# Maxima six steps ahead of the cubics, their rows in four transfers, other set-up order, fills at a step's end

## The reference

```python
mod = (silu(c) @ wmod).reshape(8, 6, 1, -1)          # sa, ca, ga, sb, cb, gb
h = layernorm(x) * (1 + ca) + sa
q, k, v = split(h @ w_qkv.T)                          # 16 heads of 8
logits = q @ k.T * 8 ** -0.5
logits = logits - max(logits, axis=-1)
s = where(x >= 0, 1 + x*(1 + x/2*(1 + x/3)), 1 / (1 - x*(1 - x/2*(1 - x/3))))   # at x = logits
x = x + ga * ((s / sum(s)) @ v @ w_out.T + b_out)
h = layernorm(x) * (1 + cb) + sb                      # then three layers with weights of +1 and -1,
x = x + gb * ffn(h)                                   # 2*128 -> 512 -> 512 -> 128, relu times 2 between
```

## Time and profile before

| | us |
|---|---|
| median of 3 runs | 708.13 (706.61 to 709.72) |
| the profiled execution, its own time | 708.76 |
| its span | 706.9 |
| VectorE busy | 646.2 (91%) |
| TensorE busy (matmuls, modelled ends) | 627.4 (89%) |
| ScalarE, GpSimd busy | 598.8, 599.0 (85% each) |
| granted TensorE clock, mean share of full | 0.971 |

### The profile page before, as it was taken

The page is one execution under the profiler, slowest core; times in us unless marked ns, Lnnn a source line. Parts: engine busy times, 40 slices in busy tenths (PEclk is TensorE's granted clock), DMA queues, the critical chain, the costliest instruction groups (busy, mean ns, idle before and its releaser), DMA issues.

```text
span 706.9 us, 9679 instructions
## 1 busy us (share of the span) xinstructions
PE 627.4 (89%) x3019; PEld 244.5 (35%) x3019; DVE 646.2 (91%) x768; ACT 598.8 (85%) x606; POOL 599.0 (85%) x390
## 2 busy tenths in 40 slices
PE   7577787877789999899989999899989999997798
PEld 5222222223222344233423333233423343334266
DVE  6899988989999999999999999999999999998943
ACT  2647877978899999999999989999999989998932
POOL 7769777897989999899989999899989989798920
PEclk9579999999999999999999999999999999999999
DMA  7514112141124222141224122241125112101001
GB/s 206 160 46 165 48 51 61 54 149 32 55 58 144 81 58 73 48 159 32 57 76 168 50 58 75 60 167 41 40 61 172 53 54 72 54 10 27 17 12 30
DMA packets 37783, 53.61 MB, mean 76 GB/s; under 512 B 11308, under 2 KB 20804, under 8 KB 37732
## 3 DMA queue, kind: packets, MB, share of 16 engines
q1 hardware_dynamic: 36766, 51.81, 24.1%
q10 hardware_dynamic: 966, 1.19, 0.6%
HBM read 29.17 MB, written 18.36 MB: 67 GB/s over the span
## 4 chain that ended last, share of the span: by engine, by line
PE 56%; DVE 17%; ACT 12%; issue 11%; POOL 2%; SPq 1%; DMA 1%; ACTq 0%; DVEq 0%; POOLq 0%
PE MB L515 13%; PE OP L593 12%; PE Z L561 9%; PE SA L576 8%; DVE cub L966 8%; DVE mx L975 7%; ACT sq L720 5%; ACT prob L734 4%; PE MB L528 3%; PE MB L505 2%; PE MB L612 2%; PE MB L486 1%; PE OP L443 1%; DVE st L1012 1%; PE MB L493 1%
## 5 line engine op out<-in xcount | busy, mean ns | idle before, releaser
L1201 POOL TENSOR_TENSOR cub<-cub 128x2048 f32<-128x2048 f32 x127 | 456.8, 3602 | 48.4 <-DVE cub L966 48.1
L720 ACT ACTIVATE sq<-Z,shift 128x1024 f32<-128x1024 f32 x256 | 282.3, 1116 | 58.5 <-PE Z L561 56.8
L966 DVE SCALAR_TENSOR_TENSOR cub<-sq,Z 128x1024 f32<-128x1024 f32 x256 | 309.8, 1211 | 13.0 <-ACT sq L720 12.2
L975 DVE TENSOR_REDUCE mx<-SA 128x2 f32<-128x1024 f32 x248 | 301.9, 1217 | 15.6 <-PE SA L576 12.2
L734 ACT ACTIVATE prob<-cub 128x2048 f32<-128x2048 f32 x128 | 244.3, 1910 | 0.4 <-PE OP L593 0.4
L576 PE MATMUL SA<-KH,QL 64*128 64x512 f32 x496 | 121.1, 485 | 33.4 <-DVE mx L975 29.3
L561 PE MATMUL Z<-QH,KH 64*128 64x512 f32 x512 | 128.8, 499 | 17.7 <-DVE cub L966 16.5
L593 PE MATMUL OP<-prob,Vq 128*16 128x512 f32 x1024 | 136.6, 607 | 0.0
L561 PEld LDWEIGHTS Z<-QH,KH 64*128 64x128 f32 x512 | 48.4, 185 | 197.6 <-DVE cub L966 121.6
L515 PE MATMUL MB<-hid,W 128*128 128x512 f32 x192 | 108.0, 645 | 0.0
L576 PEld LDWEIGHTS SA<-KH,QL 64*128 64x128 f32 x496 | 47.4, 187 | 111.1 <-DVE mx L975 89.4
(11 more groups left out here) (205 smaller groups left out, 501.6 us busy)
## 6 DMA issues: line engine op xcount, KB each, us to landing
QL<-parts_q SPq DMA_DIRECT2D x62, 128.0 KB, 2.6
KH<-parts_k SPq DMA_DIRECT2D x62, 128.0 KB, 2.7
QH<-parts_q SPq DMA_DIRECT2D x62, 128.0 KB, 2.7
parts_q<-SQ SPq DMA_DIRECT2D x28, 256.0 KB, 2.5
parts_k<-SK SPq DMA_DIRECT2D x28, 256.0 KB, 2.7
QH<-mp SPq DMA_DIRECT2D x253, 2.0 KB
nd<-OT SPq DMA_DIRECT2D x124, 32.0 KB
out<-y SPq DMA_DIRECT2D x7, 256.0 KB, 2.8
```

Of the source, the lines that this page charges most:

```text
L720: nc.scalar.activation(sq[:, h, :], Z[:, h, :], ACT.Square, bias=shift[:, 0:1]).then_inc(s_sq, 1)
L966: nc.vector.scalar_tensor_tensor(cub[:, m % RING, h, :], sq[:, h, :], CUB_ADD, Z[:, h, :], ALU.add, ALU.mult).then_inc(s_cv, 1)
L975: nc.vector.tensor_reduce(to, unit_bank(m, u)[:, :, :], AX_X, ALU.max).then_inc(s_mx, 1)
L1201: nc.gpsimd.tensor_tensor(ff, ff, ff, ALU.mult).then_inc(s_fp, 1)
```

## The change

- `AHEAD` is 6 instead of 7, so the maxima of a group stand one step later in relation to the cubics; `LEAD` goes from 3 to 4, which leaves the reading of q and k in the same steps. The three stages of `of_maxima` stand together round the first maxima of the step, where they were spread over it.
- The rows of maxima sit in rows 1, 33, 65, 97 of `QH` instead of 1, 3, 65, 67; four transfers of 4 KB carry them (`M_DMAS`) instead of eight of 2 KB. For the first quad the SyncE queue issues two and ScalarE two.
- `FILL`: one step fewer in batches 0 and 1, each fill now at the end of the step, and from batch 0 on it has a second matmul of 256 columns.
- Set-up: two dummy matmuls fewer at the start and two ahead of the first q; the transposes of the condition before those of the weights; wq and wk are copied before the modulation. One batch more of x's statistics on ScalarE (`ON_VECTOR` 3), its squares in four parts of five tiles in the steps -2 to 1 (`SQUARES_AT`) instead of in step -10; the last 1 MB of x is loaded after the first quad of q. The weights of the first layer are made on GpSimd instead of VectorE, and GpSimd's gates come after them and after the means; `gate_rows` is issued in step -3, not -7; the late roots of the norm in step 3 of batch 0, not in step -4.
- End: `l1_3` of batch 6 has a bank of `Z` to itself and starts in step 128, VectorE's last square moves behind a copy of that step, `xbg` and `wog` change places with `w2g`, and `pe_tail` issues the four products that add x before the pick of the last quad.

The core of the diff:

```diff
-AHEAD = 7
+AHEAD = 6
-ON_VECTOR = 4
+ON_VECTOR = 3
+SQUARES_AT = (-2, -1, 0, 1)
-M_DMAS = 8
-LEAD = 3
+M_DMAS = 4
+LEAD = 4
...
-    ("l1_2", -2, [(2, "c", 4)]), ("l1_3", -2, [(4, "b", 2), (4, "c", 2)]), ("y", -2, [(5, "c", 3), (5, "d", 1)]),
+    ("l1_3", -2, [(0, "b", 3), (0, "c", 1)]), ("l1_2", -2, [(2, "c", 4)]), ("y", -2, [(5, "c", 3), (5, "d", 1)]),
...
-FILL |= {(0, n): ("k", 2) for n in range(2, 12)} | {(0, n): ("v", 2) for n in range(12, 16)}
-FILL |= {(1, n): ("k", 3) for n in range(2, 8)} | {(1, n): ("x1", 1) for n in range(9, 12)} | {(1, 12): ("v", 3)}
+FILL |= {(0, n): ("k", 2) for n in range(2, 11)} | {(0, n): ("v", 2) for n in range(12, 16)}
+FILL |= {(1, n): ("k", 3) for n in range(2, 8)} | {(1, n): ("x1", 1) for n in range(9, 11)} | {(1, 12): ("v", 3)}
...
                     nc.tensor.matmul(MB[:, :], ident[:, :], W1f[:, n % KC, :], start=True, stop=True)
+                    if b >= 0:
+                        nc.tensor.matmul(MB[:, 0:S // 2], ident[:, :], W1f[:, n % KC, 0:S // 2], start=True, stop=True)
...
             logits(m, 1)
-            fill()
             with_v(s)
...
             logits(m + 1, 0)
             misc("d")
+            fill()
...
+            if s in SQUARES_AT:
+                if s == SQUARES_AT[0]:
                     act.wait_ge(s_mean1, 1)
+                count = (B - ON_VECTOR) * TB // len(SQUARES_AT)
+                for i in range(SQUARES_AT.index(s) * count, (SQUARES_AT.index(s) + 1) * count):
+                    mm = nc.scalar.activation(scratch(i), tile_of_x(i), ACT.Square, bias=mean1[:, i:i + 1],
+                                              accum_out=sq1[:, i:i + 1])
...
             cubic(s, 0)
             of_maxima(m, 0)
+            of_maxima(m, 1)
             maxima(m, 0)
-            of_maxima(m, 1)
+            of_maxima(m, 2)
             split(b, n)
             if b == B - 1:
                 norm_late()
             cubic(s, 1)
-            of_maxima(m, 2)
             maxima(m, 1)
...
             pool_setup(pool)
-            pool_gates(pool)
+            first_layer(pool)
             norms_of_x(pool, False)
             means_for_scalar(pool)
+            pool_gates(pool)
...
-            if b == FIRST and n == 9:
-                sp.wait_ge(s_gate, 7)
-                sp.dma_start(gate_rows, g_row).then_inc(s_gw, 16)
...
+            if b == FIRST and n == 13:
+                sp.wait_ge(s_gate, 7)
+                sp.dma_start(gate_rows, g_row).then_inc(s_gw, 16)
...
         def pe_tail(pe):
+            pe.wait_ge(s_xbg, B)
+            pe.wait_ge(s_taken["l1_3"], B - 1)
+            for t in range(TB):
+                nc.tensor.matmul(t_x1_banks[t // 2][:, t % 2, :], ident[:, :], xs[:, B - 1, t, :], start=(t % 2 == 0), stop=False,
+                                 skip_group_check=True)
+            pick_last(pe)
```

More of the change, by code:

```diff
@@ L355, in adaln_block @@
                     product(B - 1, "l1_1", B - 2): (SA[:, 1, :], product(B - 1, "y", B - 3)),
-                    product(B, "l1_3", B - 2): (SA[:, 0, :], product(B - 1, "l1_0", B - 2)),
+                    product(B, "l1_3", B - 2): (Z[:, 1, 0:S], None),
                     product(B, "y", B - 2): (SA[:, 1, :], product(B - 1, "l1_1", B - 2))}
@@ L473, in misc_product @@
                 pe.wait_ge(s_mx, 2 * GROUPS)
+            elif first and b == B:
+                pe.wait_ge(s_cv, 2 * GROUPS)
             bank4 = bank.rearrange("p (t d) -> p t d", t=TB)
@@ L900, in dve_setup @@
             last.then_inc(s_xn, 1)
+            dve.wait_ge(s_wT, 1)
+            for i, w in enumerate((wq, wk)):
+                to = w[:, :].rearrange("p (g e d r) -> p e g d r", g=NQ, e=2, d=HD)
+                of = SA[:, 0, i * D:(i + 1) * D].rearrange("p (g r e d) -> p e g d r", g=NQ, r=2, e=2)
+                for e in range(2):
+                    copy = nc.vector.tensor_copy(to[:, e], of[:, e])
+            copy.then_inc(s_wcp, 1)
             dve.wait_ge(s_modp, 1)
@@ L1063, in dve_step @@
             if b == FIRST and n == 1:
+                stats_of_x(dve, 1)
+            if b == FIRST and n == 2:
                 means_of_x(dve, 1)
-            if b == FIRST and n == 3:
-                for beta in range(2, ON_VECTOR):
-                    stats_of_x(dve, beta)
-                    means_of_x(dve, beta)
-                dve_weights(dve)
+                stats_of_x(dve, 2)
+                means_of_x(dve, 2)
         def dve_tail(dve):
@@ L1074, in dve_tail @@
             nc.vector.tensor_tensor(num[LAST:P], last_nd[:, 0, :], den[LAST:P], ALU.mult).then_inc(s_att, 1)
-            take_late(dve, B, "l1_3")
             dve.wait_ge(s_x1n, B - 1)
@@ L1277, in pool_step @@
                 normalise_x1(b - 1)
-            if b == FIRST and n == 12:
+            if b == 0 and n == 3:
                 norms_of_x(pool, True)
@@ L1374, in sp_step @@
                 need(sp, s_z, 8 * (quad - NQ + 1))
-                rows_of_maxima(sp, quad, 0, range(P // 32))
-                rows_of_maxima(sp, quad, 1, range(P // 32 if quad else 1))
+                rows_of_maxima(sp, quad, range(P // 32 if quad else 2))
             if (s + AHEAD + LEAD) % QUAD == 0 and 0 <= s + AHEAD + LEAD < GROUPS:
```

126 lines of the change are left out of this document (59 added, 67 removed).

## The result

The changed kernel takes 711.78 us (median of 8 executions, 710.54 to 713.11), the kernel before 708.12 (8 executions, 705.69 to 710.37). The ratio is 1.006, with a 95% interval of 1.0039 to 1.008: 3.7 us slower. The profiled execution has 711.21 us and a span of 709.4. The forecast was 705, with a range that ended at 711.5.

A forecast was written before the change was run, and what follows sets the result against it. VectorE, busy 91% of the span, was taken as the bound, with idle time where TensorE's clock is low. Terms 0 + 1.7 - 6.5 + 1.8 + 0 + 1.3 - 1.6 = -3.3 gave 705 us, range 700 to 711.5.

The forecast's parts named there:

- first cubic: End of set-up: gates hold the first rows of maxima, so the first cubic starts at 40.3; change 0.
- squares: Steps 0 and 1: five squares of x each delay ScalarE's squares of scores; 1.7 us later, bounds 0 and 3.8.
- fills: Batches 0 and 1: longer fills keep TensorE's clock from falling; -6.5 us, bounds 0 and -8.5.
- stages: Small VectorE steps per quad move to steps 2, 6, 10, 14; step 2's is no longer hidden; +1.8, bounds 0 and 3.
- end of the maxima: Steps 121 and 122: 2.6 us more on VectorE, about half fitting its idle time; +1.3, bounds 0 and 2.6.
- tail: Kernel's end: last product starts at 682.5, not 684.05, with two jobs moved ahead; -1.6, bounds -1 and -2.
- The bound of +2: First cubic: +2 if the load of x shares its queues with parts of k and q and lands 2 later.
- The falls of the clock: Batches 0 and 1: clock low from 92.5 to 97 and 154.5 to 157.5; expected gone with the new fills.
- batch 2's idle time as the floor: Fills in batches 0 and 1: they give back only VectorE idle time beyond batch 2's share.
- the 7.7: Batches 0 and 1: idle time the fills could give back, 5.05 - 1.4 and 6.3 - 2.3 together.
- Rows of maxima: Steady part: four transfers land before their scores, 0.4 us to spare, no TensorE wait; 0.

The follow-up runs named there:

- e1: Changed kernel with product y of batch 5 issued one to three places later in the last batch; 708.66 us, ratio to before 1.0008.
- e10: Changed kernel with maxima seven ahead again (AHEAD = 7, LEAD = 3), all else kept; 701.13 us, ratio to before 0.9905.
- e2: Changed kernel with the gate's transfer issued in step -2 behind quad 0's rows of maxima, not in step -3 ahead of them; 710.14 us, ratio to before 1.0035.
- e3: Changed kernel with the 1 MB load of x back in the set-up, ahead of q and k; 705.92 us, ratio to before 0.9973.
- e5: Changed kernel with the old fills: old steps, old place, no second matmul of 256 columns; 724.49 us, ratio to before 1.0205.
- e6: Kernel before with only the changed kernel's fills: their steps, place at a step's end and second matmul; 696.90 us, ratio to before 0.9835.
- e13: Changed kernel with maxima seven ahead (AHEAD = 7, LEAD = 3) and the old fills; 710.65 us, one execution.
- e8: Changed kernel with the three stages of the maxima spread over the step as before; 711.85 us, ratio to before 1.004.
- e4: Changed kernel with squares of x two at a time in steps -2, -1 and 2 to 9, late roots in step 12; 711.29 us, ratio to before 1.002.
- e14: Changed kernel, seven ahead, stages spread, load of x in the set-up, squares two at a time outside steps 0 and 1, late roots in step 12; 695.84 us.
- e11: Kernel before with the changed kernel's fills and its end (l1_3 bank, pe_tail, place of the last square); 695.61 us, ratio to before 0.9829.
- e7: Changed kernel without the fills' second matmul of 256 columns, their steps and place kept; 712.48 us, ratio to before 1.0062.
- e9: Changed kernel with both y of batch 5 issued later and the load of x back in the set-up; 702.23 us, ratio to before 0.9919.
- e12: Changed kernel with maxima seven ahead, stages spread as before and the load of x in the set-up; 696.20 us, ratio to before 0.9827.

## Why the prediction was wrong

By its own terms, with what the stretches say (the unit is us of the profiled execution):

| term | forecast | measured |
|---|---|---|
| first cubic | 0 (-2.7 to +2) | +3.3 |
| batches 0 and 1: squares +1.7, fills -6.5, stages +0.3 | -4.5 | -8.4 |
| batches 2 to 6: stages | +1.5 | +2.9 |
| last batch: end of the maxima | +1.3 | +6.2 |
| tail | -1.6 | -1.55 |
| sum | -3.3 | +2.5 |

**The step that failed is "End of the maxima".** It priced 2.6 us of VectorE's work, half of it hidden, and looked at VectorE alone. TensorE's product y in `SA` waits for the last maxima; moved one step later, they ended 2 us behind y's place. The work itself was priced well (1.6 in e1, in step 121, against 1.3); the wait and the lower clock behind it are 3.4 more, and 1.2 is a longer last step. That it is the one step of `AHEAD` which makes y wait e10 shows: seven ahead, y does not wait and the last batch is 5.2 shorter. How long the lower clock lasts is not settled by the wait alone: in e2 y waits 1.95 us at the same place, the clock is at 0.51 from 641 to 644.3 only, and the last batch takes 76.36, 1.0 less. The wait stands in `misc_product`, and y's step in `MISC`; the forecast asked what VectorE waits for, and not what waits for VectorE.

**The first cubic** had the right mechanism and the wrong size. The gates hold the rows, as e2 shows (2.4 to 3.2). Their chain began with a landing of 5.9 us; in its new place the load took 9.1, and KH of quad 1 came late as well, which no term had. Link by link the chain was 2.9 late at the mean, 2.5 at the scores (41.13 against 38.6) and 3.2 at the cubic. The 0.7 at the end is a misreading of its own: the forecast counted twelve maxima ahead of the cubic and yet left VectorE "nothing else" after the scores, while one of the twelve stands there. The bound of +2 stood for a late landing and was 1.3 short. With the load in its old place the set-up would have gained: e3 has the first cubic 3.8 earlier than before.

**The fills** gave far more than forecast. The falls of the clock I took from the earlier trace rows are gone: in the changed kernel it is at 1.00 from 64 to 640 us. From 75 us to the end of batch 1 the longest single wait of TensorE in e5 is 1.7 us, and yet the clock falls; matmuls at a step's end stop that. The Trainium skill's page "TensorE: Matmul & The Clock Gate", section "HAM oscillation — how this bites in real kernels", blames idle gaps of TensorE longer than that; these runs do not agree with it. My size came from batch 2's idle time as the floor (2.3 us in a batch); with the clock held and fewer dense layers the idle time of VectorE is 1.1 in batch 0 of e6 and 1.2 in batch 1. Batch 2's share of 61.56 us is also 1.7 and not the 1.4 in the sum, which makes 7.4 of the 7.7. And it left out what six ahead costs at the lower clock (e13 against e5), for which no term stood. Against the kernel before the two make -8.4: in the profiled executions 16.0 gained and 7.6 lost, with e5 taken at its median 12.7 gained and some 4.6 lost. That the sum came out no further off than it did is thus in part luck: terms that were too small on both sides.

**Stages of the maxima**: right in place and sign, low in size. Steps 2, 6 and 10 of a batch are 0.4 longer, steps 5, 9 and 13 give back 0.2, 0.58 in all and not 0.3. I had let steps 5, 9 and 13 give back all. e10 says that nearly all of it is the one step of AHEAD, not that the stages stand together.

**Rows of maxima**: right, no wait in the steady part. The slack is about 0.8 rather than 0.4 (e8). The issue of a transfer of 4 KB took 0.57 against 0.54 for one of 2 KB. By the Trainium skill's page "DMA: Bandwidth & Descriptors", section "Measured (HBM→SBUF, 128 partitions, SWDGE, issued from GpSimd)", small transfers are dominated by their descriptors; the time to issue does not show it, and how long the transfers themselves took no row tells. **Squares of x**: not settled, 0.9 in e4 and 2.3 in e14 against 1.7, with as much variation between profiles of the same code. **Tail**: -1.55 as forecast, and partly by luck, as only some 1.0 belongs to it (e11); the rest is that after a long last step (5.04 us against 3.81 before) less is left for the end. This step comes and goes with a fall of the clock and not with the change: e6 has it too (the clock at 0.66 from 645.6 to 650.6), e1 and e11 do not.

Left open: why the clock falls in the last steps of the last batch in some of these kernels and not in others with the same code there (before and e6).

## What to carry to other kernels

When work is moved by a step, look for every wait on its last instance, not only for those in the steady loop: here one that had been free cost 3.4 us in one place. Compare medians before trusting the stretches of one profile: e5's was 3 us over its median, and a fifth of the fills' 16.0 was that. Price a load in its new place with a range as wide as its measured landings, and with all that stands behind it. And test the parts of such a change one by one: the fills alone, in the kernel before, made it 1.65% faster, and the rest of the change turned that into 0.6% slower.

## What the runs showed of the hardware

- TensorE's clock follows small shifts of the same work. A fill of 512 columns moved from the middle to the end of a step (and one fill fewer in each batch) took batches 0 and 1 from 170.8 to 156.9 us, and the median from 724.49 to 712.48 (e5, e7). In the changed kernel an idle stretch of 1.96 us went with the 0.50 level from 641 to 647; in e2 one of 1.95 at the same place was followed by 3.3 us of it, in e1 one of 0.63 (after one of 0.82) by 3 us.
- The 1 MB load of x landed after 5.9 to 6.2 us in the kernel before and the two built on it (e6, e11), after 7.5 to 8.3 in the four changed kernels that have it in its old place in the set-up (e3, e9, e12, e14), and after 7.5 to 9.1 in the nine that have it in its new place. In the changed kernel it was 9.1, with a DMA share of 0.96 from 18 to 22 us.
- Issuing a small transfer took the SyncE queue 0.54 us for 2 KB and 0.57 us for 4 KB (batch 3, step 6); with four transfers instead of eight it was 2.27 us instead of 4.34.
